# Loading and preparing the weights of a two-layer graph attention kernel in the order of their first use

## The reference

```python
h = jnp.maximum(_layernorm(x, axis=-1), 0.0)
x = x + _L0_gnn_ref(h, Wq, bq, Wk, bk, Wv, bv, Wf, bf, adj)
    # 6 heads of 64: softmax(q k^T / 8 + (0 where adj else -9e15)) v, then @ Wf + bf
h = jnp.maximum(_layernorm(x, axis=-1), 0.0)
x = x + _L1_gnn_ref(h, adj, W, b, w_src, w_dst, H_w, H_b)
    # 12 heads of 32: heads = h @ W; th = tanh(heads)
    # attn = leaky(th.w_src + (th.w_dst)^T), masked, softmax; out = elu(attn @ heads + b)
    # gate = sigmoid(h @ H_w.T + H_b); gate * out + (1 - gate) * h
```

## Time and profile before

| | |
|---|---|
| median of 3 runs | 1394.42 us (1394.37 to 1395.95) |
| profiled execution, its own time | 1395.05 us |
| its span in the trace | 1393.1 us |
| PE busy | 1302.0 us, 93% |
| ACT busy | 1261.6 us, 91% |
| DVE busy | 1221.0 us, 88% |
| POOL busy | 904.1 us, 65% |

### The profile page before, as it was taken

How to read it: one execution, slowest core, us unless ns; L and a number is a source line. 1 busy time by engine, 2 the same in 40 slices (tenths; PEclk the granted TensorE clock), 3 DMA queues, 4 the chain that set the end, 5 groups by cost and what they waited for, 6 DMA issues and landing times.

```text
span 1393.1 us, 39297 instructions
## 1 busy us (share of the span) xinstructions
PE 1302.0 (93%) x10502; PEld 908.3 (65%) x10502; DVE 1221.0 (88%) x4457; ACT 1261.6 (91%) x3731; POOL 904.1 (65%) x1106
## 2 busy tenths in 40 slices
PE   2889999999999999999999999999999999999974
PEld 1567667766666776666677676767667666666642
DVE  3569999989898998989899898999989899999875
ACT  4469999989999999999999999999999999999975
POOL 3357777657766666777766676766667676567743
PEclk8899999999999999999999999999999999999986
DMA  5000000000000000000000000000000000000000
GB/s 151 13 14 15 26 13 27 27 26 14 26 25 13 25 25 26 14 26 15 23 25 25 15 25 26 12 26 25 25 15 25 25 14 26 25 25 3 13 13 24
DMA packets 29845, 33.28 MB, mean 24 GB/s; under 512 B 10464, under 2 KB 29664, under 8 KB 29664
## 3 DMA queue, kind: packets, MB, share of 16 engines
q1 hardware_dynamic: 29664, 31.62, 7.4%
HBM read 19.03 MB, written 12.58 MB: 23 GB/s over the span
## 4 chain that ended last, share of the span: by engine, by line
PE 48%; issue 15%; ACT 15%; DVE 14%; POOL 3%; DVEq 2%; DMA 1%; ACTq 0%; SPq 0%; POOLq 0%
PE job L501 14%; PE pt L574 10%; PE unit L550 7%; PE job L637 5%; DVE unit L986 4%; ACT p L755 4%; PE job L515 4%; ACT p L712 3%; PE job L489 3%; DVE y L993 3%; PE job L592 2%; ACT o1m L773 1%; ACT c L724 1%; DVE bn L868 1%; POOL xn L1115 1%
## 5 line engine op out<-in xcount | busy, mean ns | idle before, releaser
L755 ACT ACTIVATE p<-y,min 128x256 f32<-128x256 f32 x768 | 394.5, 537 | 10.2 <-DVE min L993 10.1
L986 DVE SCALAR_TENSOR_TENSOR unit<-unit,s,dst 128x256 f32<-128x256 f32 x768 | 336.6, 484 | 37.8 <-ACT p L755 33.6
L574 PE MATMUL pt<-ident,p 128*128 128x128 f32 x2304 | 356.6, 280 | 9.4 <-ACT p L755 5.6
L574 PEld LDWEIGHTS pt<-ident,p 128*128 128x128 f32 x2304 | 266.0, 142 | 84.5 <-issue 45.3
L501 PE MATMUL job<-w,h 128*128 128x384 f16 x1728 | 303.9, 328 | 0.9 <-DVE h L884 0.6
L993 DVE CUSTOM_DVE_ANT_0 y<-unit,mask 128x256 f32<-128x256 f32 x768 | 291.6, 417 | 0.3 <-issue 0.2
L1124 POOL TENSOR_SCALAR p<-p,rec 128x256 f32<-128x256 f32 x384 | 188.3, 506 | 116.1 <-DVE rec L927 111.5
L501 PEld LDWEIGHTS job<-w,h 128*128 128x128 f16 x1728 | 167.2, 98 | 107.9 <-DVE h L884 5.6
L763 ACT ACTIVATE pT<-pt 128x512 f32<-128x512 f32 x384 | 230.2, 621 | 7.4 <-issue 6.6
L712 ACT ACTIVATE p<-y,min 128x256 f32<-128x256 f32 x384 | 191.0, 503 | 37.5 <-PE pt L574 24.6
L515 PE MATMUL job<-h,w 128*128 128x256 f16 x1728 | 216.6, 274 | 1.4 <-DVE h L884 1.4
(11 more groups left out here) (109 smaller groups left out, 2234.0 us busy)
## 6 DMA issues: line engine op xcount, KB each, us to landing
xb<-in_x_dram SPq DMA_DIRECT2D x32, 384.0 KB, 3.3
out_dram<-y SPq DMA_DIRECT2D x32, 384.0 KB, 2.5
pT<-in_w_all_dram SPq DMA_DIRECT2D x4, 576.0 KB, 10.4
adj_raw<-in_adj_dram SPq DMA_DIRECT2D x32, 64.0 KB, 1.9
prod<-in_w_all_dram SPq DMA_DIRECT2D x1, 576.0 KB, 5.0
p<-in_w_all_dram SPq DMA_DIRECT2D x1, 576.0 KB, 11.0
out_row<-in_bf_dram SPq DMA_DIRECT2D x1, 192.0 KB, 4.1
gate_b_row<-in_gate_b_dram SPq DMA_DIRECT2D x1, 192.0 KB, 6.2
```

The costliest lines, as they stand in the source:

```text
L574: last = nc.tensor.transpose(pt_ps[u % 2][:, (2 * hh + kt) * P:(2 * hh + kt + 1) * P], probs[:, u % 3, hh, kt * P:(kt + 1) * P], ident[:])
L755: last = op(p1[:, u % 3, hh, :], y1[:, u % YB, hh, :], ACT.Exp, bias=min1[:, u, hh:hh + 1], scale=-1.0, accum_out=sum1[:, t, h:h + 1])
L986: V.scalar_tensor_tensor(leaky[:, hh * T:(hh + 1) * T], bank[:, hh * T:(hh + 1) * T], s8[par][:, t, h:h + 1], dst5[:, c % 2, hh, :], ALU.a ...
```

## The change

The loads, constants and preparations at the head of the program are put in another order; no arithmetic of a batch changes, and the loop is the same.

- SP: the three bias columns are loaded behind the first batch's x, then WF and WV; adj of batch 0 and x of batch 1 come next, and only then the five rows that are broadcast to all partitions, WH and WG.
- POOL: `pick` is made after the second `partition_all_reduce` and has a semaphore of its own (`s_pick`; `s_pool_const` now ends at 4 instead of 8). The three `largest_sums` stand ahead of iteration -2, behind it, and behind iteration -1; they stood ahead of it twice and behind it once.
- ACT: of the weights, only WQ and WK are summed ahead of the batches. High parts of WQ and WK and sums of WF and WV stand behind LN_T0 of batch 0, high parts of WF and WV behind Q 0, sums of WH and WG behind Q 2, and their high parts behind EXP0 5 in iteration 0.
- DVE: the first `scales` stand behind STATS0 of batch 0, the low parts of WQ and WK and the second `scales` behind LN_T0, the low parts of WF and WV behind K 1, the third `scales` behind K 2 and ahead of SCORES0, the low parts of WH and WG behind PV0 1 in iteration 0, and `gate_bias` behind AGGREGATE1 in iteration 0.
- PE: the value bias row is made ahead of V instead of at the start.

```diff
             def load_weight(w):
                 sp.dma_start(stage[w], w_v[w]).then_inc(s_w[w], 16)
 
-            def load_others():
-                for dst, src in small:
-                    sp.dma_start(dst, src).then_inc(s_small, 16)
-                for w in (WF, WV, WH, WG):
+            def load_columns():
+                for dst, src in columns:
+                    sp.dma_start(dst, src).then_inc(s_columns, 16)
+                for w in (WF, WV):
+                    load_weight(w)
+
+            def load_rows():
+                for dst, src in rows:
+                    sp.dma_start(dst, src).then_inc(s_rows, 16)
+                for w in (WH, WG):
                     load_weight(w)
...
-            pe.wait_ge(s_w[WF], 16)
-            pe.wait_ge(s_bvw, 1)
-            for c in range(NC):
-                last = mm(pt_ps[0][:, 0:H], bv_w[:, c, :], stage[WF][:, c, :], start=c == 0, stop=c == NC - 1)
-            last.then_inc(s_row, 1)
-            pe.wait_ge(s_pool_const, 8)
+            def value_bias_row():
+                pe.wait_ge(s_w[WF], 16)
+                pe.wait_ge(s_bvw, 1)
...
             def v(b, par, t):
+                if b.ref == 0 and t == 0:
+                    value_bias_row()
...
             for w in (WQ, WK):
                 sum_weight(w)
-            for w in (WF, WV):
-                sum_weight(w)
-            for w in (WQ, WK, WF, WV):
-                high_weight(w)
-            for w in (WH, WG):
-                sum_weight(w)
...
             def ln_t0(b, par, k):
                 high_part(made(b, "LN_T0", k)[0], h16[0], k).then_inc(s_hi0, 1)
+                if b.ref == 0 and k == 1:
+                    high_weight(WQ)
+                    high_weight(WK)
+                    sum_weight(WF)
+                    sum_weight(WV)
...
             def q(b, par, p):
-                if b.ref == 0 and p == 1:
-                    high_weight(WH)
-                    high_weight(WG)
                 bank, taken = made(b, "Q", p)
                 op(qT[par][:, p, :], bank[:, 0:T], ACT.Identity, bias=bq_c[:, p:p + 1],
                    scale=post_q[:]).then_inc(taken, 1)
+                if b.ref == 0 and p == 0:
+                    high_weight(WF)
+                    high_weight(WV)
+                if b.ref == 0 and p == 2:
+                    sum_weight(WH)
+                    sum_weight(WG)
...
                 last.then_inc(s_e0, 1)
+                if b.ref == 0 and u == 5:
+                    high_weight(WH)
+                    high_weight(WG)
...
             def aggregate1(b, par, _):
                 aggregate(b, 1, "STATS1", 1)
+                if b.ref == 0:
+                    gate_bias()
...
-                if b.ref == 0 and p == 0:
+                if b.ref == 0 and p == 1:
+                    next_weights()
+                if b.ref == 0 and p == 2:
+                    scale_rows()
                     scales(WH // 2)
-                if b.ref == 0 and p == 1:
-                    low_weight(WH)
-                    low_weight(WG)
-                    gate_bias()
...
                 V.tensor_tensor(c16[:, 1, p, :], bank[:, 0:T], c16[:, 0, p, :], ALU.subtract).then_inc(taken, 1)
+                if b.ref == 0 and p == 1:
+                    low_weight(WH)
+                    low_weight(WG)
...
-            for i in range(3):
-                G.affine_select(out=pick[:], in_=pick[:], compare_op=ALU.not_equal, fill=1.0, base=-H1 * i,
-                                pattern=[[-1, H1], [0, P]], channel_multiplier=1).then_inc(s_pool_const, 1)
-                pool.wait_ge(s_pool_const, 5 + i)
-
+            pool.wait_ge(s_pool_const, 3)
+            G.tensor_copy(ident_b[:], ident[:]).then_inc(s_pool_const, 1)
+
+            def make_pick():
+                for i in range(3):
+                    pool.wait_ge(s_pick, 1 + i)
+                    G.affine_select(out=pick[:], in_=pick[:], compare_op=ALU.not_equal, fill=1.0, base=-H1 * i,
+                                    pattern=[[-1, H1], [0, P]], channel_multiplier=1).then_inc(s_pick, 1)
...
             largest_sums(0)
             for i in range(2):
                 G.memset(ndT[i][:], 0.0)
-            G.tensor_copy(ident_b[:], ident[:]).then_inc(s_pool_const, 1)
-            largest_sums(1)
...
-                 {-2: lambda: largest_sums(2)})
+                 {-2: lambda: (largest_sums(1), make_pick()), -1: lambda: largest_sums(2)})
```

More of the change, by code:

```diff
@@ L298, in build @@
         s_w = [sem(f"s_weight{i}") for i in range(6)]
-        s_small = sem("s_small_inputs")
+        s_columns = sem("s_bias_columns")
+        s_rows = sem("s_row_inputs")
         s_wsum = sem("s_weight_sums")
@@ L305, in build @@
         s_pool_const = sem("s_pool_const")
+        s_pick = sem("s_pick")
         s_bvw = sem("s_bvw")
@@ L404, in _ @@
         def _(sp):
[L405 to L409, removed]
+            columns = [(bq_c[:], bq), (bk_c[:], bk), (bv_c[:], bv)]
+            rows = [
+                (out0_row[:], bf.partition_broadcast(P)), (src_row[:], w_src.partition_broadcast(P)),
+                (dst_row[:], w_dst.partition_broadcast(P)), (gate_b_row[:], gate_b.partition_broadcast(P)),
+                (gat_b_row[:], gat_b.partition_broadcast(P)),
             ]
@@ L453, in _ @@
             mm = nc.tensor.matmul
-            pe.wait_ge(s_w[WF], 16)
-            pe.wait_ge(s_bvw, 1)
-            for c in range(NC):
-                last = mm(pt_ps[0][:, 0:H], bv_w[:, c, :], stage[WF][:, c, :], start=c == 0, stop=c == NC - 1)
-            last.then_inc(s_row, 1)
-            pe.wait_ge(s_pool_const, 8)
+            def value_bias_row():
+                pe.wait_ge(s_w[WF], 16)
+                pe.wait_ge(s_bvw, 1)
+                for c in range(NC):
+                    last = mm(pt_ps[0][:, 0:H], bv_w[:, c, :], stage[WF][:, c, :], start=c == 0, stop=c == NC - 1)
+                last.then_inc(s_row, 1)
+            pe.wait_ge(s_pool_const, 4)
             def first_use(b, idx, w):
@@ L554, in dst @@
             def dst(b, par, c):
+                if b.ref == 0 and c == 0:
+                    pe.wait_ge(s_pick, 4)
                 if c == 0:
@@ L790, in _, with scale_rows @@
             V = nc.vector
[L791 to L797, removed]
+            def scale_rows():
+                dve.wait_ge(s_rows, 16 * 5)
+                own(V.tensor_scalar(src_row[:], src_row[:], -(1.0 - ALPHA), None, ALU.mult))
+                own(V.tensor_scalar(dst_row[:], dst_row[:], -1.0, None, ALU.mult))
             def scales(pair):
@@ L819, in low_weight, with first_scales @@
                                        ALU.mult, ALU.subtract).then_inc(s_w16, 1)
-            def first_weights():
-                low_weight(WQ)
-                low_weight(WK)
+            def first_scales():
+                dve.wait_ge(s_columns, 16 * 3)
+                own(V.tensor_scalar(bq_c[:], bq_c[:], -1.0 / 8.0, None, ALU.mult))
+                scales(0)
+                for c in range(NC):
+                    last = V.tensor_copy(bv_w[:, c, :], bv_c[:, c:c + 1].broadcast_to([P, P]))
+                last.then_inc(s_bvw, 1)
             def next_weights():
@@ L843, in gate_bias @@
                 V.tensor_scalar(post_g[:], post[:, WG:WG + 1], 0.5, None, ALU.mult).then_inc(s_gate_b, 1)
-            scales(0)
-            scales(1)
             def aggregate(b, k, step, idx=0):
                 written = ready(dve, n_bn.after(b, step, idx))
-                dve.wait_ge(s_pool_const, 8)
+                dve.wait_ge(s_pool_const, 4)
                 dve.wait_ge(s_bn, written)
@@ L862, in stats0 @@
                 if b.ref == 0:
-                    first_weights()
+                    first_scales()
             def stats1(b, par, t):
@@ L891, in ln_t0 @@
                 if b.ref == 0 and k == 1:
-                    next_weights()
+                    low_weight(WQ)
+                    low_weight(WK)
+                    scales(1)
             def ln_t1(b, par, k):
@@ L1093, in norm0 @@
                     used = ready(pool, value)
-                pool.wait_ge(s_pool_const, 8)
+                pool.wait_ge(s_pool_const, 4)
                 pool.wait_ge(s_rstd, here)
```

32 lines of the change are left out of this document (17 added, 15 removed).

## The result

| | before | after |
|---|---|---|
| median on the same chip, 4 runs each | 1394.87 us (1394.37 to 1395.95) | 1410.57 us (1409.52 to 1413.93) |
| ratio, 95% interval | | 1.0116 [1.0097, 1.0134] |
| span of the profiled execution | 1393.1 us | 1412.1 us |

A forecast was written before the change was run, and what follows sets the result against it. PE bounds the loop, so only the head, held by POOL's library changes, could move the time: -5.7 + 14.1 + 3.4 + 1.9 = +13.7 us, predicting 1408.1 us, with an 8-in-10 range of 1401.5 to 1412.

The forecast's parts named there:

- T: The moment at which xn of batch 0 is done on POOL: 29.04 us before, forecast 23.3 us after.
- part 1: Head up to the first xn: `pick` and sums of WF, WV leave POOL's path, gain 5.7 us.
- part 2: From first xn to first scaled probabilities: POOL's library changes, `pick` and third all-reduce now lie there, loss 14.1 us.
- part 4: Preparations moved into iteration 0: low and high parts delay OUT0, loss 3.4 us; `gate_bias` delays HEADS, loss 1.9 us.
- DMA traffic stretches both early changes: Rival on POOL's first two library changes: both take 9.16 us, T = 25.6, sum +16.0, 1410.4 us; chance 15%.
- Part 3: Q, K, V preparations and value bias row behind T: costed at nothing, covered by 12.6 us before DVE's scores.
- PE's clock: Far end of the range: PE's clock, low after its longer idle time, costs 1 to 2 us more.

The follow-up runs named there:

- The extra pair: Kernel after plus a tiny tensor_scalar and a repeated all-reduce behind the third, two more library changes: 1424.31 us, ratio 1.0222, 13.7 us more than after.
- the removed one: Kernel after with WH and WG summed with WF and WV and the third all-reduce directly behind the second: 1403.11 us, ratio 1.0072, 7.5 us less than after.

## Why the prediction was right

Sign, place and mechanism were as forecast: POOL's changes of library between T and p carry the loss. The terms, in the profiled executions:

| term | forecast | trace | |
|---|---|---|---|
| part 1, T earlier | -5.7 | -3.5 | 29.04 to 25.50 |
| part 2, T to p | +14.1 | +15.1 | 23.3 to 38.4 |
| part 4, PT0 to OUT0 | +3.4 | +2.6 | 14.16 to 16.71 |
| part 4, OUT0 to HEADS | +1.9 | +3.7 | 10.42 to 14.13 |
| from HEADS to the end | 0 | +1.2 | 1315.2 to 1316.4, in a scatter of 5 |
| sum | +13.7 | +19.0 | by medians +15.7 |

**Part 1 was mis-sized by 2.2 us, and the rival "DMA traffic stretches both early changes" had it right.** The first change took 9.27 against 9.16, but the second 8.98 against 6.84, so the term that was mis-sized is the second change. The argument against that rival, that those first 2 us had shown nothing before, overlooked that the second change, begun at 13.75, now has the traffic beside more than half of it: a share of 0.77 from 15 to 20 us, then 0. Moving the loads away gave 6.78 and 6.80, moving them onto the third change gave 9.05. That rival's T was 25.6 and its time 1410.4 us; measured are 25.50 and 1410.57. That the time agrees so well is partly luck: the terms below moved too, and the two changes vary from execution to execution. In the four other traces with the same head the first took 9.46 to 10.39 and the second 7.84 to 8.22. Over all five T is 24.55 to 25.65, which is 1.25 to 2.35 us more than the 23.3 forecast.

**Part 2 held in its steps.** Forecast were T + 7.1 for the second all-reduce, T + 19.2 for the mask, T + 24.3 for the end of xn and T + 37.4 for p; they came at T + 7.0, 19.3, 24.6 and 38.4. The last step is the one off, as the change back took 7.41 instead of 6.76. The extra pair (+13.7 us) prices this part from one side; the removed one (-7.5, with 5 us given back to other work) agrees in sign. The Trainium skill, GPSIMD Engine Reference, section 2.1 (Instruction dispatch), gives some 6 us for a freshly loaded library. The unloaded changes towards the all-reduce agree, with 5.76, 5.79 and 6.04 us; those back took 6.74 to 7.63, and in DMA traffic it was 7.8 to 10.7, so there the trace decides.

**Part 3 held.** Nothing of Q, K, V or the value bias row is seen: PE waits 11.10 us for DVE's first scores. Even 4 us by which the second `scales` became slower went unnoticed.

**Part 4 was right in kind, with its sizes off both ways.** The low parts stretch PE's wait for the third c from 0.99 to 3.11 us, 2.1 instead of the 2.75 forecast; 0.44 of the rest falls into the time for which DVE waited for ACT there before. The 0.65 taken for ACT's high parts shows as the one wait of 0.60 us for ACT, right behind them. It stays, with 0.71, in the kernel whose low parts are moved away, and PT0 to OUT0 is then still 0.6 us longer than before (14.75 against 14.16). The gate rows cost 2.0 us by the experiment without them, against 1.9. The other 1.7 us between OUT0 and HEADS are the clock: OUT0 takes 4.76 us instead of 3.09, in stretches whose mean granted clock is 0.86 and 0.75, so part of them at the lower of its levels (1.2 instead of 2.4 GHz). HEADS itself takes 4.76 instead of 3.08, at 0.57 from 96 to 100 us; that lies in the stretch behind the start of HEADS. The forecast had PE's clock only as 1 to 2 us at the end of its range.

**The distance to the median.** Eight profiled executions have this wait of 3.11 to 3.12 us ahead of OUT0; in four OUT0 then took 3.08 us, in four 4.65 to 5.92. So whether the clock falls there varies, and in the profiled execution of after it fell twice, at 1.7 us each. That would account for the 3.4 us by which it lies above its median. But its other executions have no trace, and what varies by up to 5 us behind the start of HEADS is a rival for the same distance, so this stays possible and not shown.

## What to carry to other kernels

In these traces a POOL operation that changes the engine's library costs 5.8 to 7.6 us each way without DMA traffic, about 13 us for a pair that stands between two ordinary operations, and the profile shows it only as idle time that ends in "issue" or under the name of a wait long over. Before spreading such operations over a program so that each stands where it is needed, count the changes on the critical engine: two of them put together shared one pair, and replaced by a small matmul they let this same order gain 10 us where it had lost 16. Where a trace shows two long and two short idle times of one kind, look at the DMA share beside each, and price a moved one by the traffic that it will meet.

## What the runs showed of the hardware that was not expected

- **DMA traffic lengthens a change of POOL's library.** Without traffic it took 5.76 to 7.63 us. The first change of the program, nearly all of it in traffic, took 9.16 to 10.69, the second, where it lay partly in it, 7.84 to 8.98, and each under 7 where the loads came later. Why each of the two varies by 1.1 us in the same head, under much the same traffic, stays open.
- **Small operations suffer beside large ones on DVE and POOL, in both directions.** Of the five operations on 128x2 elements of the second `scales` on DVE, three took 1.46 to 1.51 us, one beside each of POOL's three selects, and the two between them 0.17; with `pick` made elsewhere all five took 0.17 again. On POOL it took 1.17 to 1.27 us instead of 0.19 beside DVE's low parts, and the selects 6.86 to 6.97 instead of 4.93 to 5.01. In these kernels the first was hidden; the second cost 1.9 us on the path with one pair fewer.
- **PE's clock after the same wait differs between executions.** Behind the wait of 3.1 us OUT0 took 3.08 us in four traces and 4.65 to 5.92 in four; behind the wait of 2.0 us HEADS took 3.08 to 3.09 us in four traces and 4.76 to 4.77 in three. Runs of one kernel lie up to 10 us apart, more than several of the differences studied here. How much of that comes from these waits is not shown: behind the start of HEADS the traces already differ by 5 us.
